# Gathering the inverse counts inside the relation loop instead of in loops of the attention and feed-forward blocks

## The reference

```python
seg = edge_type * n + dst
agg = segment_sum(x[src], seg, num_segments=N_REL * n)
cnt = segment_sum(ones, seg, num_segments=N_REL * n)
mean = agg.reshape(N_REL, n, -1) / jnp.maximum(cnt, 1.0).reshape(N_REL, n, 1)
h1 = jnp.einsum('rni,rio->no', mean, W_rel) + x @ W_root + b_rgcn
```

## Time and profile before

| what | value |
|---|---|
| median of 3 runs | 1617.39 us (1614.51 to 1620.77) |
| the profiled execution | 1618.41 us |
| its span in the profile | 1616.6 us |
| PE busy | 1232.5 us (76%) |
| DVE busy | 910.4 us (56%) |
| ACT busy | 737.3 us (46%) |
| POOL busy | 673.7 us (42%) |
| the relation loop, first to last scatter | 778.2 to 1284.3 us |

### The profile page before, as it was taken

One profiled execution on the slowest core, in us unless ns is written; L12 is line 12 of the kernel. 1 busy time (PEld: TensorE's weight loads), 2 busy tenths in 40 slices (PEclk: granted clock), 3 DMA queues, 4 the chain that ended last, 5 costly groups with the idle time before them and its releaser, 6 DMA issues. The chain is left out here.

```text
span 1616.6 us, 32695 instructions
## 1 busy us (share of the span) xinstructions
PE 1232.5 (76%) x9846; PEld 928.5 (57%) x9847; DVE 910.4 (56%) x1717; ACT 737.3 (46%) x1097; POOL 673.7 (42%) x820
## 2 busy tenths in 40 slices
PE   8997665975684179638899999999999768631992
PEld 6775555974544067427566666666666455431781
DVE  8953676876554520173666666566665367676002
ACT  8994303753113265341555554555554341222661
POOL 0086836774566213112455555555555400010330
PEclk9999775886785589859999999999999869755996
DMA  1001200002004344476789999899998866467336
GB/s 57 1 1 20 63 16 1 1 1 78 11 3 147 106 140 138 144 249 240 232 253 270 287 283 272 255 275 277 282 288 244 231 185 190 112 164 175 119 128 182
DMA packets 112001, 247.49 MB, mean 153 GB/s; under 512 B 23590, under 2 KB 48675, under 8 KB 111798
## 3 DMA queue, kind: packets, MB, share of 16 engines
q1 hardware_dynamic: 78422, 157.29, 30.2%
q0 software_dynamic: 33504, 89.21, 21.8%
HBM read 216.18 MB, written 53.64 MB: 167 GB/s over the span
## 5 line engine op out<-in xcount | busy, mean ns | idle before, releaser
L644 PE MATMUL r_pO<-ring,r_rowsT 128*128 x2520 | 422.9, 327 | 0.0
L644 PEld LDWEIGHTS r_pO<-ring,r_rowsT 128*128 128x128 f16 x2520 | 244.4, 98 | 155.2 <-issue 2.0
L1843 DVE SCALAR_TENSOR_TENSOR ring<-q_wstage,ring 128x768 f16<-128x768 f32 x198 | 175.1, 954 | 55.9 <-ACT ring L1802 54.6
L1783 POOL DMA_INDIRECT acc_dram<-r_msg,r_scol x70 | 128.9, 1842 | 159.3 <-PE r_pT L1904 104.5
L1802 ACT ACTIVATE ring<-q_wstage 128x768 f16<-128x768 f32 x198 | 148.8, 829 | 25.8 <-issue 25.8
L1831 ACT ACTIVATE r_msg<-r_pO,slot_inv 128x768 f32<-128x768 f32 x70 | 62.9, 898 | 193.2 <-PE r_pO L644 192.9
L477 POOL DMA_INDIRECT inv_col<-qinv_dram,pair_col x112 | 116.2, 1037 | 77.1 <-POOL pair_col L490 69.9
L427 POOL DMA_INDIRECT slot_dram<-table_record,table_rowi x80 | 101.9, 1274 | 102.7 <-DVE table_rowi L297 76.2
L390 PE MATMUL acc<-oh_d,oh_s 125*125 125x512 f16 (+1 forms) x800 | 134.9, 308 | 0.0
L1548 PE MATMUL f_ps<-f_down,f_hT 97*128 (+1 forms) x408 | 76.0, 338 | 48.7 <-DVE f_hT L1394 43.3
L1241 POOL DMA_INDIRECT y_dram<-f_parts,f_row x34 | 33.6, 988 | 179.5 <-ACT f_parts L1446 179.5
(11 more groups left out here) (400 smaller groups left out, 2502.6 us busy)
## 6 DMA issues: line engine op xcount, KB each, us to landing
q_wstage<-in_L_gnn_W_rel_dram SPq DMA_DIRECT2D x33, 2304.0 KB, 14.2
f_stage<-in_L_ffn_w_dram SPq DMA_DIRECT2D x16, 576.0 KB, 7.1
f_stage<-y_dram SPq DMA_DIRECT2D x10, 672.0 KB
stage<-in_L_gnn_W_dram SPq DMA_DIRECT2D x6, 768.0 KB, 5.9
q_wstage<-in_L_ffn_w_fast_dram SPq DMA_DIRECT2D x6, 768.0 KB, 5.3
q_wstage<-in_L_ffn_w_slow_dram SPq DMA_DIRECT2D x6, 768.0 KB, 7.3
q_wstage<-in_L_ffn_h_fast_dram SPq DMA_DIRECT2D x6, 768.0 KB, 9.0
f_stage<-in_L_ffn_w_fast_dram SPq DMA_DIRECT2D x8, 576.0 KB, 5.7
```

The costliest lines, as they stand in the source:

```text
L644: ins = eng.matmul(out, x, w[:, h * n:(h + 1) * n], start=first and x is xh and w is wh, stop=last and x is xl, **kw)
L1783: eng.indirect_dma_start(out=K.acc_dram[u % 2], out_offset=bass.IndirectOffsetOnAxis(ap=scol[:, u:u + 1], axis=0), in_=msg[:, u, :], in_of ...
L1843: ins_ = eng.scalar_tensor_tensor(wring[:, slot, 1, k, :], wstage[:, slot, k, :], W_SCALE, wring[:, slot, 0, k, :], ALU.mult, ALU.subtract)
```

## The change

The four calls of `gather_inverse_counts` and the function itself go, and `K.slot_inv` with them. In its place POOL's step of the relation loop gathers the inverse counts of tile t + 2 between the row gathers of tile t + 4 and the scatter of tile t, into one of four columns of `inv_col`, and ACT's message reads that column directly, after one more wait. Before the first step POOL gathers for tiles 0 to 3; the first two steps gather tiles 2 and 3 once more. With the live tiles alone, 74 gathers are made instead of 112. `slot_pair` gets two spare columns of zeros, for the tiles past the end.

```diff
+    link(eng.memset(K.slot_pair[:, T1:T1 + INV_AHEAD], 0))
+    eng.tensor_copy(K.slot_pair[:, 0:T1], tmp[:, :]).then_inc(ready, 1)
...
-            else:
-                gather_inverse_counts(K, eng, s, INV_A1, INV_G2)
...
-                gather_inverse_counts(K, eng, s, 0, INV_A1)
-            else:
-                gather_inverse_counts(K, eng, s, INV_G2, INV_A2)
...
-            if layer == 0:
-                gather_inverse_counts(K, eng, s, INV_A2, T1)
...
+def gather_inverse(K, eng, copied, gathered, t, b, count):
+
+    pair = K.slot_pair
+    eng.tensor_copy(K.pair_col[:, b:b + 1], pair[:, t:t + 1] if isinstance(t, int) else pair[:, bass.ds(t, 1)]).then_inc(copied, 1)
+    eng.wait_ge(copied, count)
+    eng.nop(nofuse=True)
+    eng.indirect_dma_start(out=K.inv_col[:, b:b + 1], out_offset=None, in_=K.qinv_dram,
+                           in_offset=bass.IndirectOffsetOnAxis(ap=K.pair_col[:, b:b + 1], axis=0)).then_inc(gathered[b], 16)
...
                 relation.gather(eng, t + AHEAD, b)
+                if first and u < UN - INV_AHEAD:
+                    eng.wait_ge(inverse_gathered[u + INV_AHEAD], 16)
+                gather_inverse(K, eng, inverse_copied, inverse_gathered, t + INV_AHEAD, (u + INV_AHEAD) % UN, t + UN + 1)
                 if first and u == 0:
                     eng.wait_ge(s["seeded"], 16)
...
             for u in range(UN):
+                gather_inverse(K, eng, inverse_copied, inverse_gathered, u, u, u + 1)
+            for u in range(UN):
                 step(u, u, True)
...
                 eng.wait_ge(s["multiplied"], t + 1)
+                eng.nop(nofuse=True)
+                landed = 16 * (1 + u // INV_AHEAD)
+                eng.wait_ge(inverse_gathered[u], landed if first else (t - u) * (16 // UN) + landed)
                 if not first:
+                    eng.nop(nofuse=True)
                     eng.wait_ge(scattered[u % 2], (t - u % 2) * 8 - 16)
                     eng.nop(nofuse=True)
-                eng.activation(msg[:, u, :].rearrange("p (h n) -> p h n", h=2), pO[u % 2][:, :, 0:HC], ACT.Copy, scale=col(K.slot_inv, t + IDX_BUFS)
+                eng.activation(msg[:, u, :].rearrange("p (h n) -> p h n", h=2), pO[u % 2][:, :, 0:HC], ACT.Copy, scale=K.inv_col[:, u:u + 1]
                                ).then_inc(s["msg_ready"], 1)
```

More of the change, by code:

```diff
@@ L32 @@
 TABLED_FIRST = 46
-INV_A1, INV_G2, INV_A2 = 52, 72, 100
-IDX_BUFS = 4
+INV_AHEAD = 2
 AHEAD = 4
@@ L678, in gat_project @@
         W = Weights(K, name + "_w", rows_view(w), B["stage"], B["wparts"])
-        s = {n: K.sem(name + "_" + n) for n in ("a_loaded", "projected", "h_ready", "ones_ready", "pair_ready", "tabled"
-                                                ) + tuple("gathered_%d" % b for b in range(IDX_BUFS))}
+        s = {n: K.sem(name + "_" + n) for n in ("a_loaded", "projected", "h_ready", "ones_ready", "tabled")}
         a_bc = B["a_bc"]
@@ L778, in gat_attend @@
         s = {n: K.sem(name + "_" + n) for n in ("cs_ready", "als_ready", "max_done", "uv_made", "uv_ready", "bc_ready", "rows_copied", "t1_ready", "arg_ready",
-                                                "e_ready", "p_ready", "pv_done", "out_free", "finish_a", "finish_b", "bias_loaded", "small_loaded", "pair_ready", "table_turned", "columns_ready"
-                                                ) + tuple("gathered_%d" % b for b in range(IDX_BUFS))}
+                                                "e_ready", "p_ready", "pv_done", "out_free", "finish_a", "finish_b", "bias_loaded", "small_loaded", "pair_ready", "table_turned", "columns_ready")}
         mx, mm, u_all, v_all, s2_all = (B["small"][:, n, 0:heads, :] for n in range(5))
@@ L1143, in ffn_phase @@
             "b2_ready", "b2_placed", "stored", "w_hi", "w_lo", "merged", "cut_hi", "cut_lo", "turned", "evicted", "up_ready", "relu_ready", "h_ready", "h_hi", "h_lo",
-            "down_ready", "y_ready", "summed", "added", "out_stored", "pair_ready") + tuple("gathered_%d" % b for b in range(IDX_BUFS))}
+            "down_ready", "y_ready", "summed", "added", "out_stored")}
         s_up = [K.sem("f%d_up_chunk%d" % (layer, c)) for c in range(UPS)]
@@ L1720, in relation_phase @@
         scattered = [K.sem("r_scattered%d" % a) for a in range(2)]
+        inverse_gathered, inverse_copied = [K.sem("r_inverse%d" % u) for u in range(UN)], K.sem("r_inverse_copied")
         block = ctx.enter_context(nc.Block())
@@ L1790, in _ @@
             pairs = live_pairs(eng)
-            times = [eng.value_load(K.live_row[0:1, 1 + half:2 + half], min_val=1, max_val=TURNS + 1) for half in range(2)]
+            times = [eng.value_load(K.live_row[0:1, 1 + half:2 + half], min_val=2, max_val=TURNS + 1) for half in range(2)]
             for a in range(2):
@@ L1795, in _ @@
                 eng.wait_ge(gathered[u], times[u // 2] * 32)
+            for u in range(UN):
+                eng.wait_ge(inverse_gathered[u], times[1 - u // 2] * 16)
             eng.nop(nofuse=True)
@@ L2124, in build @@
         K.row_move = K.sb("row_move", [128, T1 + AHEAD], FP32)
[L2125 to L2128, removed]
+        K.slot_pair = K.sb("slot_pair", [128, T1 + INV_AHEAD], I32)
+        K.pair_col = K.sb("pair_col", [128, UN], I32)
+        K.inv_col = K.sb("inv_col", [128, UN], FP32)
         K.rel_row = K.sb("rel_row", [1, T1], I32)
```

## The result

| | before | after |
|---|---|---|
| median us | 1617.97 (1614.51 to 1620.77, 4 runs) | 1638.21 (1637.23 to 1639.16, 4 runs) |
| ratio, 95% interval | | 1.0126 (1.0105 to 1.0147) |
| profiled execution, its span, us | 1618.41, 1616.6 | 1639.16, 1637.4 |
| feed-forward starts on POOL, us | 497.89 | 489.72 |
| first, fifth, last scatter of the loop, us | 778.22, 809.62, 1284.27 | 771.71, 803.73, 1306.57 |

The change makes the kernel 1.3% slower, 20 us. The prediction was 1648 us with a range of 1620 to 1680.

The account below looks back on a forecast made before the run. PE was taken to bound the loop at 7.30 us a step, with POOL taking over after the change. 1618.4 + 35.8 - 5.5 = 1648.7 us, forecast as 1648 because the profiled execution ran 1.0 above the median; range 1620 to 1680.

Parts of the forecast that it names:

- POOL's undisturbed step: Relation loop: POOL's shortest step of 5.38 us plus 1.89 for the added copy, wait and DMA gives 7.27 us.
- POOL keeps up: Rival, relation loop: POOL's step is 7.11 us, PE stays the bound, the loop costs nothing; 1612 us, chance 0.14.
- The disturbance: Relation loop: DVE's weight groups stretch POOL's operations, raising its step from 7.27 to 7.85 us.
- two ways: Pricing POOL's stretching beside DVE: from today's loop, 0.55 us a step; by operation, 0.63 us a step.
- The loop: Relation loop: 65 steps grow from 7.30 to 7.85 us each, adding 35.8 us.
- The removed gathers: End of attention: without the old loop before the barrier, feed-forward starts 5.7 us earlier; with the new memset, -5.5 us.
- The head: Ahead of the loop and its first steps: about 10 us of added gathers are covered by waits; 0, between 0 and 3.
- ACT's wait: Message in the relation loop: counts land well before ACT wants them, some 13 us after issue; cost 0.
- Copies only: Rival, relation loop: DVE's groups stretch POOL's two copies but no DMA issue; step 7.50 us, total 1626 us, chance 0.08.
- Late counts: Rival, relation loop: counts queue behind row gathers and ACT waits; step about 8.4 us, total 1684 us, chance 0.05.
- DMA as the bound: Rival, relation loop: tiny fetches overload nearly full DMA engines; 8.4 us a step, 1684 us, chance 0.03.
- Clock: Rival, relation loop: PE rests and its granted clock falls to 0.88; step 8.3 us, total 1678, chance 0.03.

Follow-up runs that it names:

- doubled: Changed kernel with a second copy and indirect DMA in each step, into spare buffers nobody reads; 1776.32 us (one run).
- idle_gather: Kernel before, old loops kept, with the new gathers added to POOL's loop but unused by ACT; 1647.49 us, ratio 1.0172.
- one_ahead: Changed kernel with the inverse counts gathered one tile ahead instead of two; 1643.46 us, ratio 1.0157.
- one_copy: Changed kernel with the same gathers but no copy of their own: their row numbers ride as a third column in the row-number copy; 1606.93 us, ratio 0.9933.
- no_counts: Changed kernel without any gathers of inverse counts, ACT's message scaled by 1; 1607.02 us, ratio 0.9938.
- barrier_only: Kernel before with old gather loop bounds 56, 76, 96 instead of 52, 72, 100, so fewer tiles before the barrier; 1619.42 us, ratio 1.0011.
- barrier_two: Kernel before with old gather loop bounds 48, 68, 92 instead of 52, 72, 100; 1607.7 us, ratio 0.9947.
- the control: Kernel before with DVE's weight group in the relation loop cut from six instructions to one; 1607.05 us, ratio 0.992.

## Why the prediction was right, and by how much its terms were off

**What bounds the loop.** Right. "POOL has room, and the question is how much" was answered with 1.92 us and a need of 1.89; in the changed kernel PE's wait before the scatter is gone and "issue" stands in its place, 19.7 us over 61 scatters.

**POOL's undisturbed step**, forecast 5.38 + 1.89 = 7.27, measured 7.15. The 1.89 was right (doubled: 1.93). The 5.38 was the mis-sized term: it rested on one place where a ready scatter started 0.46 us after the gather. After, that gap is 0.30 or 0.31 wherever nothing disturbs, and 4.92 + 0.30 + 1.89 is 7.11. The rival "POOL keeps up" had this number. The trace of before held a better measure: at the head of its loop, where messages are ready, the first scatter starts at 778.22 and the second at 783.48, 5.26 us, with a gap of 0.30. The 0.12 us are 7.8 us over 65 steps, most of the miss.

**The disturbance**, forecast 0.58 (7.85 - 7.27, between two ways that gave 0.55 and 0.63), measured 0.59. The size was right, and in part by luck: the two ways had put all of it on DVE's groups, and only 0.42 us are shown to be theirs.

**The loop**, forecast 65 x 0.55 = +35.8, measured +28.2.

**The removed gathers**, forecast -5.5, measured -8.2 at the start of feed-forward and -6.5 at the first scatter. The step "the next phase starts 494.21 - 488.50 = 5.7 us earlier" took the 3.68 us behind POOL's last copy for a constant of the barrier. It is 1.30 to 1.45 behind DVE.

**The head**, forecast 0 between 0 and 3, measured +0.6; scatter 0 still waited 6.45 us for the seeding, of 12.37 before. **ACT's wait**, forecast 0: right, by idle_gather and one_ahead. The 3.2 us that stood behind it were too short for the full loop: where ACT waited in one_ahead, landing took mostly 6 to 7.5. The lead of two tiles covers that as well. **Behind the loop** nothing was forecast, and 1.5 us went.

The sum was 1648.7 for a profiled execution that took 1639.16. The miss of 9.5 is 7.6 of the loop, 1.0 ahead of it and 1.5 behind, less the 0.6 of the head.

**The rivals.** POOL keeps up: half right in the undisturbed step, refuted by the disturbance; without a disturbance POOL's 7.15 would have been under PE's 7.30. Copies only: refuted by the stretched issues, which lose 0.29 us a step on the mean; the pair copy loses 0.25. (The prediction counted the stretched scatter of the earlier trace rows against the rule of the page. That scatter takes its row numbers from `r_scol`, so it need not speak against it.) Late counts and DMA as the bound: refuted by one_copy and no_counts. Clock: from 800 us on it read 0.97 to 1.00 (0.83 in the head, 780 to 800 us), and it did not make the step, since POOL set the pace. **The signs**: PE was forecast at 92 to 94 busy and showed 95 to 98; the last scatter was forecast at 1315 and came at 1306.57.

## What to carry to other kernels

An engine's room is its shortest step against the step of the bound, not its busy share: POOL at 57% busy had 2 us of 7.3 left, and at 71% it was the bound. Take that shortest step from a place where the engine runs back to back (the head of the loop had it), not from one row. Before moving work into a loop, look for what can carry it there for nothing: here a third column in a copy that was made anyway was the whole difference between 1.3% slower and 0.7% faster. And a loop of filler work beside a block is free only up to that block's end; when its bounds are moved, look at every block that gets more.

## What the runs showed that was not expected

- **The passage between phases depends on who is last.** With POOL last, 3.68 us from its last instruction to its first of the next phase, and 4.89 at the first barrier of barrier_only. With DVE last, 1.30 from DVE's after the change, 1.44 in barrier_two, and 0.38 at the first barrier before. Why was not tried.
- **DMA issues on POOL are stretched beside DVE's weight groups.** The scatter's issue took 1.765 us on the mean and 1.620 with the groups cut, single ones 2.28 (at 803.73 us after); the second row gather 1.129 and 1.016. In one_copy it is the inverse DMA, 1.127 against 0.96.
- **Windows of the steady part do not show the head.** PE was 99 to 100% busy from 900 to 1200 us before, and the control made its loop 11 us shorter without touching its work. 7.4 of them lie in five steps around 800 us, where a DVE group stands before the selection matrix that PE waits for.
- **Small fetches into nearly full DMA engines cost nothing that can be seen here.** 128 fetches of 4 bytes a step, at 91 to 96% DMA share, moved the step by 0.006 us (7.308 against 7.302).
